# Three fp32r products for the unshifted channels, and a denominator shared out over ScalarE and GpSimd, in a recurrent layer with a selected transformer block

## The chip, the cores and the metric

The kernel runs on one core of a Trainium2 chip. The metric is the device time of one execution in microseconds; a kernel is run several times and the median is taken. The engines are TensorE (PE, with its weight loads shown apart as PEld), VectorE (DVE), ScalarE (ACT), GpSimd (POOL) and SyncE (SP), which issues most of the transfers. Each executes its own instructions in the order in which they are written, and they wait for each other through semaphores.

## The reference, cut to what matters

The input is x of 32 sequences, 512 tokens and 256 channels. The first layer mixes each channel with a neighbour in time, but only for the lower half of the channels: `xx` equals `x` in channels 128 to 255, so that there `xk`, `xv` and `xr` are all plain `x`.

```
xx = concat([x shifted forward [:64], x shifted back [64:128], x[128:]])
xk = x * mix_k + xx * (1 - mix_k)          # xv, xr likewise
k, v, r = xk @ Wk.T, xv @ Wv.T, xr @ Wr.T
for t:                                     # w = spatial_decay / T, u = spatial_first / T
    out_t = (a + exp(u + k_t) * v_t) / (b + exp(u + k_t))
    a, b = a * exp(w) + exp(k_t) * v_t, b * exp(w) + exp(k_t)
x = layernorm(x + (sigmoid(r) * out) @ Wo.T)
```

Behind it stands a second block: a router weighs each token, the 63 heaviest tokens of each sequence go through RMS norm, attention with rotary positions and an MLP (GELU, 1024 wide), and the result is put back and normed.

## The kernel before

Channels lie on the 128 partitions in CC = 2 halves (c = 0: the shifted ones, c = 1: the unshifted ones), and the T = 512 tokens of a sequence lie along the free dimension. The kernel has three parts: a loop over the 32 sequences (to about 500 us), 16 pairs of sequences in attention (to about 728 us), and an MLP over 8 groups of tokens.

The loop is software-pipelined. Each engine has its own `period(at)`, which lists by hand what it does in the period of sequence n, for sequences n+1 down to n−3. In the words below, K, V and R are the three projections of a sequence, each in two PSUM banks.

- TensorE: `projections(n)` waits for `mixed(n)` and does K, V and R (L766): for each, two output halves by two channel halves, 12 fp32 products of 512 columns, each recorded as two instructions. Then `outputs(n-1)` waits for the gate `g_ready(n-1)`, and adds x (transposes, L779) and the output projection (L781). In some periods from n = 19 on, `selection(n)` adds small products (`weights_turn`, `slots_turn`, and `picks`, L822 and L826, in n = 28 and 29).
- ScalarE: `exp_k_of(n)`, two exponentials of K, one to SBUF (L1111), one in place in PSUM (L1113); `reciprocal_of(n-1)` (L1132) waits for `sum_done(n-1)`; `differences_scaled(n+1)` (L1140) writes three scaled copies into `xm` and signals `scaled`; `variances_of(n-2)` (L1153 to L1155); `exp_r_of(n)` (L1117); `ln_den_of(n)` (L1123); `ln_gate_of(n)` (L1127); `evacuation_of(n-1)` (L1148); `rows_of(n-3)` (L1160), which writes the normed rows.
- GpSimd: `differences_of(n+1)` (L548); `gate_of(n-1)` (L570) waits for `num_done` and `rec_done` of n−1; `mixes_of(n+1)` (L554), three additions behind `scaled(n+1)`, signals `mixed(n+1)`; `scale_of(n-2)` raises the variance to the power −1/2 (L577) and computes the offsets of the norm (L579, L580); `log_sum_of(n)` (L561).
- VectorE: `den_scan_of(n)` (L1431), two scans that give b, with the decay read from the tile `ewb`, in which exp(w) stands 512 times per channel; `den_of(n)` (L1445), two sums exp(u) · exp(k) + b; `products_of(n)` (L1438); `clamp_of(n)` (L1453); `num_of(n)` (L1458, L1463); then from n = 18 on the selection (top-k in rounds of eight, L1552 and L1554, one-hot matrices, L1590, scans with the column `ones` repeated, L1566 and L1571); then `statistics_of(n-1)` (L1472, L1483, L1487).

In attention, ScalarE and GpSimd still finish the norm of the last sequences between their other work. In the last loop period GpSimd also gathers a mask and norms the first tokens (`attention_begun`) ahead of the gate. The MLP already splits its operands into a rounded fp32r part and an fp32r rest, and does three fp32r products in place of one fp32 product (L1073, L1084).

Of the kernel before, what the change touches and what calls it, by code (L numbers as in the profile page):

```python
# [7 lines left out]
def rwkv_then_selected_block_kernel(nc, x_chan, w_attn, columns, mask_rows, positions,  # L8
# [20 lines left out]
    P = 128  # L29
# [30 lines left out]
    with ctx:  # L60
# [17 lines left out]
        ewb = sb("ewb", [P, CC, T])  # L78
# [84 lines left out]
        u_hi, u_lo = half_at(rest, FC, GP * P), half_at(rest + FC * GP * P, FC, GP * P)  # L163
        psK, psV, psR = ps[:, 0:2, :], ps[:, 2:4, :], ps[:, 4:6, :]
# [56 lines left out]
        sc = ewb.rearrange("p a (h k) -> p (a h) k", k=K)  # L221
# [38 lines left out]
        ewb_made = sem("ewb_made")  # L260
# [27 lines left out]
        t2_done = sem("t2_done")  # L288
        s2_done = sem("s2_done")
# [226 lines left out]
        def _(pool):  # L516
# [33 lines left out]
            def mixes_of(s):  # L550

                pool.wait_ge(scaled, s.n + 1)
                for m in range(3):
                    last = g.tensor_tensor(xm[s.par][:, m, :], xm[s.par][:, m, :], xs[s.k][:, :], ALU.add)  # L554
                last.then_inc(mixed, 1)

            def log_sum_of(s):
# [3 lines left out]
                g.tensor_tensor(ld[s.par][:, :, :], ld[s.par][:, :, :], er[s.par][:, :, :], ALU.add).then_inc(sum_done, 1)  # L561

# [85 lines left out]
            def period(at):  # L648
# [98 lines left out]
        def _(pe):  # L747
# [350 lines left out]
        def _(act):  # L1098
# [790 lines left out]
```

## Time and profile before

| What | Value |
|---|---|
| Median of 3 runs | 848.66 us (844.45 to 848.79) |
| The profiled execution | 843.93 us |
| Its span, first to last instruction | 841.9 us |
| Mean granted clock of TensorE | 0.963 |
| Busy: PE, DVE, ACT, POOL | 774.4, 677.3, 497.2, 508.8 us |

The busy times are unions over the whole span, so they average over the three parts of the kernel. The profiled execution is one run; the times of the rows come from it alone, and it is 4.7 us under the median of the others.

### The profile page before, as it was taken

What the parts mean: (1) busy time and instruction counts of PE and PEld (TensorE: products, weight loads), DVE (VectorE), ACT (ScalarE), POOL (GpSimd) and SP (SyncE); (2) the same over time, 40 slices, a digit from 0 to 9 for tenths busy, and PEclk for the clock granted to TensorE, in tenths of its full rate; (3) what the DMA queues carried; (4) which work ended last, traced back from release to release, by engine and by line L of the source; (5) the groups of instructions that cost most, each with busy time, mean ns of one, the idle gap of its engine ahead of it and who ended that gap; (6) DMA issues with size and microseconds to landing.
All of it is one profiled execution on the core that took longest, in us unless ns stands there. A gap on an engine that the chain in (4) does not pass through costs nothing.

```text
span 841.9 us, 12743 instructions
## 1 busy us (share of the span) xinstructions
PE 774.4 (92%) x4276; PEld 524.8 (62%) x4276; DVE 677.3 (80%) x1382; ACT 497.2 (59%) x908; POOL 508.8 (60%) x463
## 2 busy tenths in 40 slices
PE   6899999999999999999999986779998898899982
PEld 4455556565555556455456654567776777899982
DVE  5788988888888899999998996698698664258873
ACT  2557777868777786877765664555565666322210
POOL 1677878787887868788675894455464633102223
PEclk8999999999999999999999999899899997999996
DMA  8023242322223242232321111501010110000001
GB/s 218 1 62 114 63 126 62 111 76 95 92 69 119 62 122 67 87 102 63 110 78 63 44 57 54 160 27 45 26 36 22 39 52 2 1 1 14 26 26 37
DMA packets 37335, 55.37 MB, mean 66 GB/s; under 512 B 3360, under 2 KB 26528, under 8 KB 37280
## 3 DMA queue, kind: packets, MB, share of 16 engines
q1 hardware_dynamic: 34464, 46.28, 18.2%
q0 software_dynamic: 2816, 8.39, 3.3%
q8 instruction: 31, 0.51, 0.3%
q14 instruction: 24, 0.20, 0.1%
HBM read 35.78 MB, written 18.87 MB: 65 GB/s over the span
## 4 chain that ended last, share of the span: by engine, by line
PE 62%; DVE 21%; issue 7%; POOL 5%; ACT 3%; DMA 1%; SPq 0%; POOLq 0%; DVEq 0%; ACTq 0%
PE ps L766 26%; PE ps L781 9%; PE ps L1084 6%; PE ps L1073 6%; DVE arena L1431 3%; PE ps L961 2%; PE ps L779 2%; PE ps L894 2%; DVE arena L1483 2%; DVE arena L1463 2%; DVE arena L1458 2%; PE ps L969 2%; DVE arena L1453 2%; DVE arena L1472 2%; DVE ps L1438 1%
## 5 line engine op out<-in xcount | busy, mean ns | idle before, releaser
L766 PE MATMUL ps<-arena,wa 128*128 128x512 f32 x768 | 340.5, 599 | 9.9 <-DMA wa<-w_attn 5.1
L766 PEld LDWEIGHTS ps<-arena,wa 128*128 128x128 f32 x768 | 146.9, 192 | 184.4 <-issue 168.4
L781 PE MATMUL ps<-wa,arena 128*128 128x256 f32 x512 | 131.7, 380 | 0.0
L570 POOL TENSOR_TENSOR arena<-arena 128x1024 f32<-128x1024 f32 x32 | 75.8, 2367 | 87.2 <-issue 64.5
L554 POOL TENSOR_TENSOR arena<-arena 128x512 f32<-128x512 f32 x93 | 115.9, 1275 | 5.8 <-ACT arena L1140 5.8
L1431 DVE TENSOR_TENSOR_SCAN arena<-ewb,ps 128x511 f32<-128x511 f32 x64 | 74.5, 1205 | 24.5 <-ACT ps L1113 23.3
L781 PEld LDWEIGHTS ps<-wa,arena 128*128 128x128 f32 x512 | 87.3, 190 | 6.6
L561 POOL TENSOR_TENSOR arena<-arena 128x1024 f32<-128x1024 f32 x32 | 75.7, 2366 | 15.8 <-ACT arena L1127 15.8
L1458 DVE TENSOR_TENSOR_SCAN arena<-ewb,ps 128x511 f32<-128x511 f32 x64 | 74.1, 1199 | 0.0
L1160 ACT ACTIVATE arena<-arena 128x256 f32<-128x256 f32 x128 | 66.0, 589 | 0.0
L1117 ACT ACTIVATE ps<-ps 128x1024 f32<-128x1024 f32 x32 | 32.3, 1008 | 55.9 <-PE ps L766 55.9
L1140 ACT ACTIVATE arena<-arena,cols 128x512 f32<-128x512 f32 x93 | 60.0, 710 | 0.0
L577 POOL TENSOR_TENSOR arena<-arena,mhalf 128x8 f32<-128x8 f32 x32 | 53.2, 1661 | 7.5 <-ACT arena L1155 5.8
L627 POOL TENSOR_SCALAR arena<-arena,norm 128x256 f32<-128x256 f32 x16 | 15.3, 954 | 67.8 <-ACT norm L1255 67.7
L1453 DVE TENSOR_SCALAR arena<-ps 128x1024 f32<-128x1024 f32 x32 | 39.1, 1222 | 20.9 <-ACT ps L1117 20.9
L1339 ACT ACTIVATE arena<-ps 128x512 f32<-128x512 f32 x32 | 19.1, 598 | 61.1 <-PE ps L1073 61.1
L740 POOL TENSOR_TENSOR fst<-fst,mhalf 128x2 f32<-128x2 f32 x8 | 5.7, 716 | 81.7 <-DVE fst L1847 81.7
L779 PEld LDWEIGHTS ps<-ident,arena 128*128 128x128 f32 x256 | 35.9, 141 | 26.8 <-issue 15.8
L1084 PE MATMUL ps<-halves 128*128 128x256 f32 x384 | 49.0, 289 | 3.7 <-DVE halves L1818 3.7
L1111 ACT ACTIVATE arena<-ps 128x1024 f32<-128x1024 f32 x32 | 32.7, 1023 | 33.0 <-PE ps L766 33.0
L1084 PEld LDWEIGHTS ps<-halves 128*128 128x128 f32 x384 | 48.1, 198 | 3.9 <-DVE halves L1818 3.9
L779 PE MATMUL ps<-ident,arena 128*128 128x128 f32 x256 | 48.9, 273 | 0.5 <-POOL arena L570 0.5
(215 smaller groups left out, 1523.2 us busy)
## 6 DMA issues: line engine op xcount, KB each, us to landing
arena<-x_chan SPq DMA_DIRECT2D x32, 512.0 KB, 4.1
out<-arena SPq DMA_DIRECT2D x32, 512.0 KB, 3.3
arena<-x_chan SPq DMA_DIRECT2D x64, 127.8 KB, 3.3
wa<-w_attn SPq DMA_DIRECT2D x1, 1024.0 KB, 7.7
wa<-w_up SPq DMA_DIRECT2D x1, 1024.0 KB, 6.1
wa<-w_down SPq DMA_DIRECT2D x1, 1024.0 KB, 5.5
wqk<-w_qk SPq DMA_DIRECT2D x1, 512.0 KB, 4.8
wv<-w_v SPq DMA_DIRECT2D x1, 256.0 KB, 5.0
```

What stands on the lines that cost most here:

```text
L554: last = g.tensor_tensor(xm[s.par][:, m, :], xm[s.par][:, m, :], xs[s.k][:, :], ALU.add)
L561: g.tensor_tensor(ld[s.par][:, :, :], ld[s.par][:, :, :], er[s.par][:, :, :], ALU.add).then_inc(sum_done, 1)
L570: g.tensor_tensor(gg[s.par][:, :, :], num[s.par][:, :, :], ld[s.par][:, :, :], ALU.mult).then_inc(g_ready, 1)
L766: last = mm(bank[:, o, :], wa[:, m, c, o * P:(o + 1) * P], rhs, start=(c == 0), stop=(c == CC - 1))
L779: mm(psY[:, j, c * P:(c + 1) * P], xc[s.k][:, c, tokens], ident[:, :], is_transpose=True, start=(c == 0), stop=False)
L781: last = mm(psY[:, j, :], gg[s.par][:, c, tokens], wa[:, 3, c, :], start=False, stop=(c == CC - 1))
L1084: last = mm(ps[:, 4 + g.par, i * C:(i + 1) * C], x[:, f, i * P:(i + 1) * P], w[:, f, :], start=(f == 0 and t == 0), stop=(f == FC - 1 and ...
L1140: last = a.activation(xm[s.par][:, m, :], diff[:, :], ACT.Copy, scale=mix[:, m:m + 1])
L1160: last = a.activation(xt[s.k][:, j, :], xt[s.k][:, j, :], ACT.Identity, scale=stat[s.par][:, j, S2:S2 + 1], bias=nm[s.par][:, j:j + 1])
L1431: last = v.tensor_tensor_scan(bb[:, c, 1:T], ewb[:, c, 0:T - 1], psK[:, c, 0:T - 1], 0.0, ALU.mult, ALU.add)
L1453: v.tensor_scalar(er[s.par][:, :, :], psR[:, :, :], 2.0 ** 62, None, ALU.min).then_inc(clamp_done, 1)
L1458: v.tensor_tensor_scan(aa[:, c, 1:T], ewb[:, c, 0:T - 1], psV[:, c, 0:T - 1], 0.0, ALU.mult, ALU.add).then_inc(scan_a_done, 1)
```

## The change

It has five parts.

1. For the unshifted half (c = 1), which all three projections read as plain x, the weights and x are split into a part rounded to fp32r and the rest: `w1_hi` (ScalarE) and `w1_lo` (VectorE) once, `x1_hi` (ScalarE, in `differences_scaled`) and `x1_lo` (GpSimd, behind the three mixes, carrying the `mixed` signal now) for each sequence. One fp32 product becomes three fp32r products: hi·hi, hi·lo, lo·hi. Sequence 0 keeps the fp32 product. The half c = 0 stays fp32.
2. The power −1/2 of the norm is no longer GpSimd's `pow` but ScalarE's logarithm and exponential (`logs_of`, `roots_of`).
3. The second half of the denominator is taken from VectorE: ScalarE multiplies exp(k) by exp(u) (`den_part_of`, behind the reciprocal), and GpSimd adds b (`den_second_of`, between `gate_of` and `mixes_of`). `ln_den_of` waits for both halves. VectorE's next denominator scan waits for GpSimd's addition.
4. The scans read the decay as one column repeated (`euw[:, 1, c:c+1].to_broadcast`), and the tile `ewb` is gone; its place in SBUF (`late`) holds the product of part 3, and later the scores.
5. GpSimd does `scale_of` after `log_sum_of`, no longer before it.

```diff
 mixes_of (GpSimd)
                 for m in range(3):
-                    last = g.tensor_tensor(xm[s.par][:, m, :], xm[s.par][:, m, :], xs[s.k][:, :], ALU.add)
-                last.then_inc(mixed, 1)
+                    g.tensor_tensor(xm[s.par][:, m, :], xm[s.par][:, m, :], xs[s.k][:, :], ALU.add)
+                g.tensor_tensor(x1_lo[s.par], xc[s.k][:, 1, :], x1_hi[s.par].bitcast(fp32), ALU.subtract).then_inc(mixed, 1)
...
+            def den_second_of(s):
+                pool.wait_ge(eku_done, s.n + 1)
+                pool.wait_ge(scan_b_done, s.n + 1)
+                if s.had(2):
+                    pool.wait_ge(ld_done, s.n - 1)
+                g.tensor_tensor(den[s.par][:, 1, :], eku[:, :], bb[:, 1, :], ALU.add).then_inc(den1_done, 1)
...
 scale_of (GpSimd)
-                pool.wait_ge(t2_done, s.n + 1)
-                g.tensor_tensor(stat[s.par][:, :, S1:S2 + 1], stat[s.par][:, :, VE:VN + 1], mhalf[...], ALU.pow).then_inc(s2_done, 1)
...
 period (GpSimd)
                 if at.had(1) and at.back(1).exists():
                     gate_of(at.back(1))
+                if at.exists():
+                    den_second_of(at)
                 if nxt.exists():
                     mixes_of(nxt)
-                if at.had(2) and at.back(2).exists():
-                    scale_of(at.back(2))
                 if isinstance(at.n, int) and at.n == B - 1:
                     value_tiles_cleared()
                 if at.exists():
                     log_sum_of(at)
+                if at.had(2) and at.back(2).exists():
+                    scale_of(at.back(2))
...
 projections (TensorE)
                     for o in range(CC):
-                        for c in range(CC):
-                            rhs = xm[s.par][:, m, :] if c == 0 else xc[s.k][:, c, :]
-                            last = mm(bank[:, o, :], wa[:, m, c, o * P:(o + 1) * P], rhs, start=(c == 0), stop=(c == CC - 1))
+                        out_part = slice(o * P, (o + 1) * P)
+                        mm(bank[:, o, :], wa[:, m, 0, out_part], xm[s.par][:, m, :], start=True, stop=False)
+                        if isinstance(s.n, int) and s.n == 0:
+                            last = mm(bank[:, o, :], wa[:, m, 1, out_part], xc[s.k][:, 1, :], start=False, stop=True)
+                            continue
+                        for t, (w, x) in enumerate(((w1_hi, x1_hi), (w1_hi, x1_lo), (w1_lo, x1_hi))):
+                            last = mm(bank[:, o, :], w[:, m, out_part], x[s.par], start=False, stop=(t == 2))
...
+            def den_part_of(s):
+                act.wait_ge(ek_done, s.n + 1)
+                if s.had(1):
+                    act.wait_ge(den1_done, s.n)
+                a.activation(eku[:, :], ek[:, 1, :], ACT.Copy, scale=euw[:, 0, 1:2]).then_inc(eku_done, 1)
...
 ln_den_of (ScalarE)
                 act.wait_ge(den_done, s.n + 1)
+                act.wait_ge(den1_done, s.n + 1)
...
 differences_scaled (ScalarE)
                 for m in range(3):
-                    last = a.activation(xm[s.par][:, m, :], diff[:, :], ACT.Copy, scale=mix[:, m:m + 1])
-                last.then_inc(scaled, 1)
+                    a.activation(xm[s.par][:, m, :], diff[:, :], ACT.Copy, scale=mix[:, m:m + 1])
+                a.activation(x1_hi[s.par], xc[s.k][:, 1, :], ACT.Copy).then_inc(scaled, 1)
...
+            def logs_of(s):
+                act.wait_ge(t2_done, s.n + 1)
+                if s.had(2):
+                    act.wait_ge(rows_done, s.n - 1)
+                a.activation(stat[s.par][:, :, S1:S2 + 1], stat[s.par][:, :, VE:VN + 1], ACT.Ln).then_inc(logs_done, 1)
+            def roots_of(s):
+                act.wait_ge(logs_done, s.n + 1)
+                a.activation(stat[s.par][:, :, S1:S2 + 1], stat[s.par][:, :, S1:S2 + 1], ACT.Exp, scale=-0.5).then_inc(s2_done, 1)
...
 period (ScalarE)
                 if at.had(1) and at.back(1).exists():
                     reciprocal_of(at.back(1))
+                if at.exists():
+                    den_part_of(at)
                 if at.back(-1).exists():
                     differences_scaled(at.back(-1))
                 if at.had(2) and at.back(2).exists():
                     variances_of(at.back(2))
                 if at.exists():
                     exp_r_of(at)
+                if at.had(2) and at.back(2).exists():
+                    logs_of(at.back(2))
+                if at.exists():
                     ln_den_of(at)
+                if at.had(2) and at.back(2).exists():
+                    roots_of(at.back(2))
...
 attention (ScalarE, n == 1)
                     variances_of(At(0, B - 1))
                     rows_of(At(0, B - 3))
+                    logs_of(At(0, B - 1))
                     rows_of(At(0, B - 2))
+                    roots_of(At(0, B - 1))
...
 den_scan_of and den_of (VectorE)
+                if s.had(1):
+                    dve.wait_ge(den1_done, s.n)
...
-                    last = v.tensor_tensor_scan(bb[:, c, 1:T], ewb[:, c, 0:T - 1], psK[:, c, 0:T - 1], 0.0, ALU.mult, ALU.add)
+                    last = v.tensor_tensor_scan(bb[:, c, 1:T], euw[:, 1, c:c + 1].to_broadcast([P, T - 1]), psK[:, c, 0:T - 1], 0.0, ALU.mult, ALU.add)
...
-                for c in range(CC):
-                    last = v.scalar_tensor_tensor(den[s.par][:, c, :], psK[:, c, :], euw[:, 0, c:c + 1], bb[:, c, :], ALU.mult, ALU.add)
-                last.then_inc(den_done, 1)
+                v.scalar_tensor_tensor(den[s.par][:, 0, :], psK[:, 0, :], euw[:, 0, 0:1], bb[:, 0, :], ALU.mult, ALU.add).then_inc(den_done, 1)
```

## Rows read from the trace of the kernel before

**Rows 1.** The page's busy times (us, share of the span, instructions).

```profile
PE 774.4 (92%) x4276; PEld 524.8 (62%) x4276; DVE 677.3 (80%) x1382; ACT 497.2 (59%) x908; POOL 508.8 (60%) x463
```

**Rows 2.** Timeline of PE: start us, us, line, operation, count.

```profile
203.92 10.46 PE L766 MATMUL ps<-arena,wa 128*128 128x512 f32 x24
...
218.55 10.46 PE L766 MATMUL ps<-arena,wa 128*128 128x512 f32 x24
```

**Rows 3.** The chain that ended last, first and last of 17 equal blocks.

```profile
43.08 10.30 PE ps L766 x24
...
277.26 10.31 PE ps L766 x24
```

**Rows 4.** Busy time by stretch: PE, PEld, DVE, ACT, POOL, granted clock, DMA.

```profile
57.71:277.25 219.54, 219.54 (x722) 124.31 (x721) 188.95 (x391) 165.21 (x251) 173.61 (x136) 1.00 0.30 91
...
415.75:427.00 11.25, 11.25 (x40) 6.68 (x40) 10.97 (x24) 7.30 (x12) 9.50 (x8) 1.00 0.41 119
448.54:452.00 3.46, 3.46 (x6) 1.52 (x6) 3.30 (x14) 0.00 (x0) 0.47 (x1) 0.56 0.75 233
```

**Rows 5.** Timeline of ACT, DVE and POOL in the period of rows 2.

```profile
207.55 1.02 ACT L1111 ACTIVATE arena<-ps 128x1024 f32<-128x1024 f32 x1 [0.36 <-PE ps L766]
...
209.52 2.33 DVE L1431 TENSOR_TENSOR_SCAN arena<-ewb,ps 128x511 f32<-128x511 f32 x2 [0.97 <-ACT ps L1113]
...
210.45 1.94 ACT L1140 ACTIVATE arena<-arena,cols 128x512 f32<-128x512 f32 x3
210.76 2.36 POOL L570 TENSOR_TENSOR arena<-arena 128x1024 f32<-128x1024 f32 x1 [2.97 <-ACT arena L1132]
...
213.08 3.74 POOL L554 TENSOR_TENSOR arena<-arena 128x512 f32<-128x512 f32 x3
```

**Rows 6.** Timeline at the start of the loop.

```profile
22.82 3.72 POOL L554 TENSOR_TENSOR arena<-arena 128x512 f32<-128x512 f32 x3 [5.77 <-ACT arena L1140]
...
26.59 3.70 PE L766 MATMUL ps<-arena,wa 128*128 128x512 f32 x8 [0.88 <-POOL arena L554]
```

**Rows 7.** The chain that ended last, single steps of several lines.

```profile
400.76 1.21 DVE wseq L1566
...
445.74 0.44 PE ps L822 x4
...
460.72 0.87 PE ps L781 x4
...
752.06 5.76 PE ps L1084 x48
```

**Rows 8.** Groups by line: count, busy us, mean ns, idle before.

```profile
L554 POOL TENSOR_TENSOR arena<-arena 128x512 f32<-128x512 f32 x93 | 115.9, 1275 | 5.8 <-ACT arena L1140 5.8
...
L1445 DVE SCALAR_TENSOR_TENSOR arena<-ps,euw,arena 128x512 f32<-128x512 f32 x64 | 45.1, 746 | 3.2
```

**Rows 9.** Timeline of PE, the projections of sequences 28 and 31.

```profile
429.05 10.57 PE L766 MATMUL ps<-arena,wa 128*128 128x512 f32 x24
...
482.43 10.46 PE L766 MATMUL ps<-arena,wa 128*128 128x512 f32 x24
```

**Rows 10.** The chain that ended last, denominator scans, first and last of ten.

```profile
299.88 2.34 DVE arena L1431 x2
...
389.20 2.34 DVE arena L1431 x2
...
406.06 2.34 DVE arena L1431 x2
...
438.08 2.34 DVE arena L1431 x2
```

**Rows 11.** Timeline of DVE in the selection.

```profile
416.38 2.17 DVE L1571 TENSOR_TENSOR_SCAN wseq<-ones,wseq 16x512 f32<-16x512 f32 x1
```

**Rows 12.** Timeline of POOL in attention.

```profile
513.18 1.68 POOL L577 TENSOR_TENSOR arena<-arena,mhalf 128x8 f32<-128x8 f32 x1 [5.83 <-ACT arena L1155]
...
525.20 1.68 POOL L577 TENSOR_TENSOR arena<-arena,mhalf 128x8 f32<-128x8 f32 x1 [1.70 <-ACT arena L1160]
```

More of the change, by code:

```diff
@@ L77, in rwkv_then_selected_block_kernel @@
         euw = sb("euw", [P, 2, CC])
-        ewb = sb("ewb", [P, CC, T])
+        late = sb("late", [P, CC, T])
+        eku = late[:, 0, :]
         rwb = sb("rwb", [P, C])
@@ L163, in rwkv_then_selected_block_kernel @@
         u_hi, u_lo = half_at(rest, FC, GP * P), half_at(rest + FC * GP * P, FC, GP * P)
+        at_x = rest
+        x1_hi, x1_lo = ([halves[:, at_x + (2 * n + i) * T:at_x + (2 * n + i + 1) * T] for i in range(2)] for n in range(2))
+        w1_hi, w1_lo = (halves[:, at_x + 4 * T + n * 3 * C:at_x + 4 * T + (n + 1) * 3 * C].rearrange("p (m o) -> p m o", o=C) for n in range(2))
         psK, psV, psR = ps[:, 0:2, :], ps[:, 2:4, :], ps[:, 4:6, :]
@@ L220, in rwkv_then_selected_block_kernel @@
         kblk = [place(CC, 2 * P) for _ in range(2)]
-        sc = ewb.rearrange("p a (h k) -> p (a h) k", k=K)
+        sc = late.rearrange("p a (h k) -> p (a h) k", k=K)
         pT = both(H // 2, P)
@@ L288, in rwkv_then_selected_block_kernel @@
         t2_done = sem("t2_done")
+        logs_done = sem("logs_done")
+        den1_done = sem("den1_done")
+        eku_done = sem("eku_done")
+        w1_rounded = sem("w1_rounded")
+        w1_split = sem("w1_split")
         s2_done = sem("s2_done")
@@ L572, in scale_of @@
             def scale_of(s):
-                pool.wait_ge(t2_done, s.n + 1)
                 if s.had(2):
                     pool.wait_ge(rows_done, s.n - 1)
-                g.tensor_tensor(stat[s.par][:, :, S1:S2 + 1], stat[s.par][:, :, VE:VN + 1], mhalf[:, 0:2 * TJ].rearrange("p (j a) -> p j a", a=2), ALU.pow).then_inc(s2_done, 1)
                 pool.wait_ge(s2_done, s.n + 1)
@@ L756, in projections @@
                 pe.wait_ge(mixed, s.n + 1)
+                if isinstance(s.n, int) and s.n == 1:
+                    pe.wait_ge(w1_split, 1)
                 for m, bank, ready, used in ((0, psK, k_ready, den_done), (1, psV, v_ready, num_done), (2, psR, r_ready, clamp_done)):
@@ L1105, in _ @@
             act.wait_ge(consts_made, 4)
+            act.wait_ge(w_in, 16)
+            a.activation(w1_hi, wa[:, 0:3, 1, :], ACT.Copy).then_inc(w1_rounded, 1)
             def exp_k_of(s):
@@ L1110, in exp_k_of @@
                     act.wait_ge(ekv_done, s.n)
+                    act.wait_ge(eku_done, s.n)
                 a.activation(ek[:, :, :], psK[:, :, :], ACT.Exp).then_inc(ek_done, 1)
                 a.activation(psK[:, :, :], psK[:, :, :], ACT.Exp).then_inc(ekp_done, 1)
+            def den_part_of(s):
[3 more added lines that the diff above has]
+                a.activation(eku[:, :], ek[:, 1, :], ACT.Copy, scale=euw[:, 0, 1:2]).then_inc(eku_done, 1)
             def exp_r_of(s):
@@ L1326, in _ @@
             variances_of(At(0, B - 2))
+            logs_of(At(0, B - 2))
+            roots_of(At(0, B - 2))
             for n in range(1, NP + 4):
@@ L1419, in _ @@
             dve.wait_ge(rw_chain, 3)
-            dve.wait_ge(ewb_made, 1 + CC)
             dve.wait_ge(first_col, 2)
+            dve.wait_ge(w1_rounded, 1)
+            v.tensor_tensor(w1_lo, wa[:, 0:3, 1, :], w1_hi.bitcast(fp32), ALU.subtract).then_inc(w1_split, 1)
             def den_scan_of(s):
                 dve.wait_ge(ekp_done, s.n + 1)
+                if s.had(1):
+                    dve.wait_ge(den1_done, s.n)
                 if s.had(2):
@@ L1443, in den_of @@
                 dve.wait_ge(scan_b_done, s.n + 1)
-                for c in range(CC):
-                    last = v.scalar_tensor_tensor(den[s.par][:, c, :], psK[:, c, :], euw[:, 0, c:c + 1], bb[:, c, :], ALU.mult, ALU.add)
-                last.then_inc(den_done, 1)
+                v.scalar_tensor_tensor(den[s.par][:, 0, :], psK[:, 0, :], euw[:, 0, 0:1], bb[:, 0, :], ALU.mult, ALU.add).then_inc(den_done, 1)
             def clamp_of(s):
@@ L1457, in num_of @@
                 for c in range(CC):
-                    v.tensor_tensor_scan(aa[:, c, 1:T], ewb[:, c, 0:T - 1], psV[:, c, 0:T - 1], 0.0, ALU.mult, ALU.add).then_inc(scan_a_done, 1)
+                    v.tensor_tensor_scan(aa[:, c, 1:T], euw[:, 1, c:c + 1].to_broadcast([P, T - 1]), psV[:, c, 0:T - 1], 0.0, ALU.mult, ALU.add).then_inc(scan_a_done, 1)
                 if s.had(2):
```

4 lines of the change are left out of this document (removed).

## The prediction

> **What bounds the kernel now.** I read the page's totals first: TensorE (PE) is busy 92% of an 841.9 us span [rows 1]. That is an average over a recurrent loop (to about 500 us), attention (to 728) and the MLP, and the change touches almost only the loop, so I read one period of the loop. In the PE timeline the 24 projection matmuls of one sequence start at 203.92 and those of the next at 218.55 [rows 2], and the chain that ended last holds such blocks 14.64 us apart from 43 us on [rows 3]: (277.26 − 43.08)/16 = 14.636. The granted clock is 1.00 with PE busy all 219.54 us of that stretch [rows 4]. So the first half of the loop is pure PE time: 24 × 0.4287 = 10.29 (the block's 10.30) and 4.34 for the outputs. From n = 19 the selection's small VectorE (DVE) operations join in and the chain runs over DVE; K(28) starts at 429.05 [rows 9], 152.0 after K(18) at 277.06 (K(n) is the first projection matmul of sequence n).
>
> PE is not the only loop, though. mixed(n) starts K(n); K(n)'s bank lets ScalarE (ACT) do two exponentials and then `reciprocal_of(n-1)`; that lets GpSimd (POOL) do `gate_of(n-1)`, and behind it, in order, stand `mixes_of(n+1)`, which start K(n+1). In the same period: K at 203.92, ACT's first exponential at 207.55, the gate at 210.76, the mixes from 213.08 for 3.74, so to 216.82 [rows 2, 5]. That is 12.90, and PE takes up K(n+1) only at 218.55. The start of the loop shows this circle when PE does wait for it: mixes end at 22.82 + 3.72 = 26.54, K(1) starts at 26.59, 0.05 later [rows 6]. So the circle is 12.95 against PE's 14.64: 1.7 us in reserve, and it is what the change spends.
>
> **The change, part by part, for one period.**
>
> *Projections.* Half of the twelve fp32 products (12 of 24 instructions, 12 × 0.4287 = 5.14) become 18 fp32r products over 512 columns. No row shows one. In the MLP 48 fp32r products over 256 columns take 5.76 [rows 7], 0.120 each; a product over 512 columns is surely not shorter, so 0.120 is the floor and 0.240 (twice that) the ceiling. An fp32 instruction over 512 columns, which takes 0.4287, is a second neighbour: fp32 over 256 columns takes 0.87/4 = 0.217 [rows 7], 1.8 times the fp32r one, so 0.4287/1.8 = 0.238, or with exactly half 0.214. Small products of 16 columns pace at 0.44/4 = 0.11 [rows 7], so part of the 0.120 is weight loading, which 512 columns would hide. I take 0.220, near the half. PE's period: 14.64 − 5.14 + 18 × 0.220 = 13.46. K alone: 8 × 0.4287 = 3.43 becomes 4 × 0.4287 + 6 × 0.220 = 3.03, so 0.40 off the circle (0.27 to 0.43; 1.0 at the floor).
>
> The Trainium skill (TensorE: Matmul & The Clock Gate, section Back-to-back issue gap) gives 131 ns for a matmul of 512 columns in a sustained stream of weight load and matmul. The rows speak against it here: 256 columns alone take 0.120. By it K would take 2.50 and the circle below would be 0.53 shorter.
>
> *POOL.* Two operations are put on the circle. `den_second_of(n)` stands between gate and mixes: one 128x512 add, 1.24 (a mix takes 1275 ns, three of them 3.74, overlapping a little [rows 5, 8]). `x1_lo` stands behind the three mixes and carries `mixed` now: another 1.25. The `pow` of L577 (1.68) goes, but it stood behind the mixes, as log_sum does: that takes nothing off the circle.
> Neither wait of `den_second_of` ends late: scan_b ends some 2.4 after ACT's second exponential, the gate 3.6 after it.
>
> The Trainium skill (GPSIMD Engine Reference, section Engine selection) sends a two-input elementwise add to VectorE. The rows bear that out, 746 ns there against 1275 [rows 8]; by the rule the second half of the denominator would have stayed and the circle been 1.24 shorter.
>
> *ACT.* `den_part_of` and `x1_hi` are 0.65 each (three scalings take 1.94 [rows 5]), logs and roots about 0.1 to 0.2 each. Counted from the first exponential of K(n), L1140 begins at 2.90 and ends at 4.84; with both additions `scaled` comes at 6.14, and POOL reaches the mixes at 3.21 + 2.32 (the gate) + 1.24 = 6.77. They fit, with 0.6 us left. The whole engine: 165.21/15 = 11.0 busy per period before [rows 4], 12.6 after, under 15; POOL's 11.6 becomes 12.4. Ln, Exp and Copy alternate already in each period with no table load between, so I price none.
>
> *DVE.* One of two 746 ns sums goes: −0.70. The scan's repeated column replaces a tile: I price it at nothing; such a scan with `ones` took 1.21 us [rows 7], two of L1431 2.33 [rows 5]. DVE is busy 188.95 of 219.54 here [rows 4], idle 2.0 per period, 0.97 of it before the scan [rows 5], so the gain is hidden in the first half. Where DVE sets the pace, nine periods take 438.08 − 299.88 = 138.2 from scan to scan, 15.36 each, and the longest 16.86 (389.20 to 406.06) [rows 10].
>
> **The sum.** New circle: 12.95 − 0.40 (K) + 1.24 (den_second) + 1.25 (x1_lo) = 15.04, say 15.05. It exceeds PE's 13.46 and the old 14.64: the loop changes its bound from PE to POOL and each period grows by 0.41.
> Start: period 0 keeps fp32, ACT's exponentials end at 20.81, den_part takes 0.65, but POOL's den_second waits for the scan, which ended at 23.35, then 1.24 + 3.72 + 1.25: K(1) at 29.65 for 26.59. K(2) at 44.70 for 42.91: +1.8.
> To K(18): 16 × 0.41 = +6.6, so +8.4 in all.
> K(18) to K(28): 10 × 15.05 = 150.5. Without the 0.70 DVE's mean there is 14.66, under the circle, but the load is uneven (the longest still 16.16, 1.1 over), and what the long periods exceed is not given back by the short ones; between 0 and 4 us in all I take 2.5: 153.0 for 152.0, +1.0.
> K(28) to K(31) was 53.4 [rows 9], 17.8 a period, since `picks` lie on PE in two of them. There PE still binds and gains its 14.64 − 13.46 = 1.18; the third goes by the circle, as long as it was. The granted clock fell behind the picks (0.56 in 448.54 to 452 [rows 4]) and should again: −2.4.
> Tail: in period 31 POOL's mask gather and norms stand ahead of the gate and are pushed about 0.6 back by the later log_sum. In attention the two `pow` on the chain (513.18, 525.20 [rows 12]) go. The first saves 1.1 (1.68 for two short ACT operations). The second loses 0.8: the roots of sequence 31 now stand behind another `rows_of`, 2.0 of ACT. Net +0.3.
> 8.4 + 1.0 − 2.4 + 0.3 = +7.3: span 849.2. The profiled execution took 843.93, 2.0 over its span, so 851.2. The median of the runs is 848.66, 4.7 above that execution, for a cause no view shows; the lowest is 844.45. On the median the sum gives 856.0, and that is my time.
>
> **Rivals.**
> 1. *PE stays the bound* (faster). It decides if the circle is under 13.5, so 1.55 less than summed: as if den_second and one mix cost nothing. Then 13.46 for 14.64 over 26 periods, about −30 + a few for DVE's stage: 820 to 825. For it: PE's 92%. Against: the circle's 12.95 already stands before 2.49 of POOL is added. Chance 0.06.
> 2. *fp32r products of 512 columns near the floor* (no change or a little faster). At 0.120 K takes 2.43, the circle 14.45: −0.2 for +0.41 per period, 26 × 0.6 = 16 less: about 840. By the 131 ns that the Trainium skill's page (TensorE: Matmul & The Clock Gate, Back-to-back issue gap) states it would be 842. At least 10 us come off once a product takes under 0.155. Against: the 0.217 and 0.120 at 256 columns. Chance 0.06. That some other link of the circle is 0.3 shorter than summed (POOL's semaphore handling) gives 848: 0.08.
> 3. *Worse than the circle.* ACT's `scaled` misses its 0.6 us, POOL's adds meet two-input DVE work (once a scan with both inputs in SBUF took 2.17 for 1.21, beside a POOL add [rows 11]), or PE, idle for 1.6 us in each period, is granted the lower clock now and then: K at 1.2 GHz costs 3.0 more. A wait of PE of 1.7 just before 415.75 left the clock at 1.00 [rows 4], so few: 0.3 to 1 us per period, 863 to 880. Chance 0.12.
> 4. *The change does not do what it says*: if fp32r over 512 columns takes 0.4287 as fp32, PE's period is 17.2 and the time about 920. Chance 0.02.
>
> **How the numbers follow.** The likeliest, POOL's circle at 14.95 to 15.2 with 0 to 4 for DVE's stage and the runs' own spread of 4.5, holds 0.66 and reaches from 847 to 863. To leave out no more than 2 in 10 the range takes the near parts of rivals 2 and 3: 845 to 865. A measurement of this kernel can tell about 0.5%, 844.4 to 852.9. Slower: most of the likeliest, rivals 3 and 4, 0.65. Same: the low end of the likeliest and the 0.08 of rival 2, 0.24. Faster: rival 1 and the floor of rival 2 in most of its width, 0.11.
>
> **What the profile of the changed kernel would show.** Right: K blocks 15.05 apart up to n = 25, PE idle about 1.6 before each with POOL's last `mixes_of` line named as releaser, PE's busy share down to about 85%, POOL's operations from gate to x1_lo back to back (8.5 us), K's bank ready some 3.3 after its start. The fp32r products should pace at 0.214 to 0.24. Wrong: K blocks waiting for ACT or DVE, a gap between gate and den_second (a late scan), or between den_second and the mixes (a late `scaled`); PE without idle time at 13.5 would mean rival 1.

## The result, and the profile after

| | before | after |
|---|---|---|
| median of the runs compared (us) | 846.56 (844.05 to 848.79, 4 runs) | 864.55 (862.92 to 867.14, 4 runs) |
| profiled execution / its span (us) | 843.93 / 841.9 | 862.92 / 861.2 |
| K(n) to K(n+1), median of the periods from K(2) to K(18) (us) | 14.64 | 15.16 |

The ratio is 1.0216 [1.0167, 1.0265]: slower, by 1.7 to 2.7%. The forecast was 856.0, in 845 to 865.

As in the prediction, K(n) is the first projection matmul of sequence n, and period n runs from K(n) to K(n+1). DVE's stage is K(18) to K(28), in which VectorE also does the selection.

The page's busy times, after:

```profile
PE 754.7 (88%) x4462; PEld 560.8 (65%) x4462; DVE 665.7 (77%) x1348; ACT 538.9 (63%) x1036; POOL 536.9 (62%) x494
```

Against [rows 1] PE lost 19.7 us of work, POOL and ACT gained 28.1 and 41.7, and the span still grew by 19.3: the work taken off PE did not set the time. One period of the first half shows why. This is the timeline of all engines after, for the period that answers to [rows 2, 5] (lines left out lie on engines that end early):

```profile
194.28 1.12 PE L783 MATMUL ps<-arena,wa 128*128 128x512 f32 x2 [1.24 <-POOL halves L563]
...
199.55 1.14 ACT L1165 ACTIVATE arena<-arena,lnbias 128x1024 f32<-128x1024 f32 x1
...
200.91 2.37 POOL L586 TENSOR_TENSOR arena<-arena 128x1024 f32<-128x1024 f32 x1 [2.82 <-ACT arena L1165]
...
203.04 0.62 ACT L1174 ACTIVATE halves<-arena 128x512 fp32r<-128x512 f32 x1
203.25 1.27 POOL L577 TENSOR_TENSOR arena<-late,arena 128x512 f32<-128x512 f32 x1
...
204.48 3.75 POOL L562 TENSOR_TENSOR arena<-arena 128x512 f32<-128x512 f32 x3
...
208.18 1.27 POOL L563 TENSOR_TENSOR halves<-arena,halves 128x512 fp32r<-128x512 f32 x1
...
209.51 1.12 PE L783 MATMUL ps<-arena,wa 128*128 128x512 f32 x2 [1.30 <-POOL halves L563]
```

Read it as a circle: K starts at 194.28; ACT's reciprocal (L1165) starts 5.27 later; the gate (L586), `den_second` (L577), the mixes (L562) and `x1_lo` (L563) stand one behind the other on POOL from 200.91 to 209.45 without a gap; K(n+1) starts 0.06 behind them. Before each K, PE idles 1.2 to 1.3, and L563 is named as its releaser. `x1_hi` (L1174), with which ACT signals `scaled`, ends at 203.66, before the mixes begin.

In the second half the same circle breaks now and then. PE's timeline after, at K(19) and at the three K that come late:

```profile
300.43 1.12 PE L783 MATMUL ps<-arena,wa 128*128 128x512 f32 x2 [1.23 <-POOL halves L563]
...
316.92 2.07 PE L783 MATMUL ps<-arena,wa 128*128 128x512 f32 x2 [2.12 <-POOL halves L563]
...
351.17 2.07 PE L783 MATMUL ps<-arena,wa 128*128 128x512 f32 x2 [3.57 <-POOL halves L563]
...
431.26 2.08 PE L783 MATMUL ps<-arena,wa 128*128 128x512 f32 x2 [3.99 <-POOL halves L563]
```

POOL's timeline after, ahead of the first late K, and one line of a later place (L569 log_sum, L556 differences, L586 gate, L577 `den_second`):

```profile
300.32 2.37 POOL L569 TENSOR_TENSOR arena<-arena 128x1024 f32<-128x1024 f32 x1
...
303.06 1.32 POOL L556 TENSOR_TENSOR arena<-arena 128x512 f32<-128x512 f32 x1
306.97 2.39 POOL L586 TENSOR_TENSOR arena<-arena 128x1024 f32<-128x1024 f32 x1 [2.59 <-issue]
310.65 1.27 POOL L577 TENSOR_TENSOR arena<-late,arena 128x512 f32<-128x512 f32 x1 [1.29 <-issue]
...
431.18 2.34 POOL L569 TENSOR_TENSOR arena<-arena 128x1024 f32<-128x1024 f32 x1
```

DVE's timeline after, in the same two places (L1560 and L1563 weigh the tokens, L1621 chooses the slots, L1523 is statistics, L1484 the scan of the denominator):

```profile
300.61 2.22 DVE L1560 TENSOR_TENSOR weights<-stats_all 128x64 f32<-128x64 f32 x1
...
303.27 1.20 DVE L1563 TENSOR_SCALAR weights<-weights,rbb 128x64 f32<-128x64 f32 x1
...
305.00 1.40 DVE L1523 BATCH_NORM_STATS2 arena<-arena 128x6 f32<-128x256 f32 x4
...
308.19 2.33 DVE L1484 TENSOR_TENSOR_SCAN arena<-euw,ps 128x511 f32<-128x511 f32 x2
...
431.46 2.60 DVE L1621 SCALAR_TENSOR_TENSOR wseq<-wsrc,topv,wseq 16x512 f32<-16x512 f32 x1
```

The gate ends at 309.36, but `den_second` starts at 310.65: it waits for the scan, which ends at 310.52. The scan is late because DVE's selection operations and statistics stand ahead of it, and two of the former were long: L1560 took 2.22 and L1563 1.20, while the next operation of L1560's shape, L1561, took 0.28, and L1563's counterpart before 0.28. Both end about 0.1 after the POOL operation beside them: 302.83 against 302.69, 304.47 against 304.38. L1621 too took 2.60, beside L569 and the small operation behind it; 0.73 before.

Such meetings are not new. The kernel before, at K(19) (PE, then DVE, then POOL's gate):

```profile
291.74 10.46 PE L766 MATMUL ps<-arena,wa 128*128 128x512 f32 x24
...
293.32 1.10 DVE L1509 TENSOR_TENSOR weights<-stats_all 128x64 f32<-128x64 f32 x1
...
299.88 2.33 DVE L1431 TENSOR_TENSOR_SCAN arena<-ewb,ps 128x511 f32<-128x511 f32 x2
...
298.50 2.37 POOL L570 TENSOR_TENSOR arena<-arena 128x1024 f32<-128x1024 f32 x1 [2.94 <-issue]
```

The same add took 1.10 and ended 0.14 after POOL's log_sum, which ended at 294.28. The scan began 8.14 after K(19) and ended at 302.21, 1.34 after the gate (300.87). In after it begins 7.76 behind K(19). So the scan is no later against its K than it was; what is new is that POOL, and with it K(n+1), waits for it. The other two late places are alike: the scans of 21 and 26 begin 8.8 and 9.2 behind their K in after, 9.5 and 10.3 before.

The Trainium skill (SBUF — State Buffer, section SBUF: two separate sides) says that a DVE operation with two SBUF inputs and a GpSimd operation that reads SBUF exclude each other for the whole instruction, and that one in a 2-port perf mode is shut out in the same way. The trace agrees for two inputs, 2.22 for 0.28 beside POOL's 2.37. L1563 has one tensor and a column as inputs and was held as well; in which mode it ran, no view shows.

The windows behind each late K (us, busy of PE, PEld, DVE, ACT, POOL, then the granted clock, DMA share, GB/s), and the first half of the loop:

```profile
316.92:320.30 3.38, 3.38 (x6) 2.06 (x7) 3.28 (x9) 1.18 (x4) 3.38 (x4) 0.51 0.51 155
320.30:324.00 3.70, 3.70 (x13) 2.17 (x12) 2.10 (x15) 2.03 (x3) 0.40 (x1) 0.99 0.73 212
351.17:354.30 3.13, 3.13 (x5) 1.83 (x6) 3.06 (x9) 0.69 (x2) 3.13 (x4) 0.50 0.48 150
...
431.26:434.40 3.14, 3.14 (x5) 1.83 (x6) 3.10 (x3) 0.71 (x2) 3.14 (x4) 0.50 0.47 148
...
57.69:280.00 222.31, 204.75 (x790) 136.44 (x791) 174.63 (x371) 180.36 (x306) 181.21 (x146) 1.00 0.30 90
```

PE idle for 1.2 to 1.3 in every period keeps 2.4 GHz over the whole first half; behind idle times of 2.12, 3.57 and 3.99 it works at 1.2 GHz (0.51, 0.50, 0.50) for over 3 us.

**Where the 19.3 us are.** K(18) starts at 285.28, 8.2 later than before (277.10). K(18) to K(28): 285.28 to 448.91 = 163.6, 11.7 more (before: 277.10 to 429.05 = 151.95). K(28) to K(31): 50.8, 2.6 less. K(31) to the end: 861.2 − 499.73 = 361.5, 2.0 more. That is 19.3. Each of these figures comes from one execution.

### The profile page after: what moved, and what is told of

Its sections match the earlier page's. It is cut to its first block and busy times, and to the rows that moved or that the text cites. A ratio compares the mean times of both kernels' runs of the same rounds, so it can differ in the third digit from the quotient of the medians.

```text
span 861.2 us, 13340 instructions
## 1 busy us (share of the span) xinstructions
PE 754.7 (88%) x4462; PEld 560.8 (65%) x4462; DVE 665.7 (77%) x1348; ACT 538.9 (63%) x1036; POOL 536.9 (62%) x494
## 5 line engine op out<-in xcount | busy, mean ns | idle before, releaser
L783 PE MATMUL ps<-arena,wa 128*128 128x512 f32 x384 | 205.3, 617 | 46.9 <-POOL halves L563 43.7
L788 PE MATMUL ps<-halves 128*128 128x512 f32 x558 | 240.0, 539 | 0.0
L788 PEld LDWEIGHTS ps<-halves 128*128 128x128 f32 x558 | 108.2, 194 | 101.1 <-issue 92.5
L586 POOL TENSOR_TENSOR arena<-arena 128x1024 f32<-128x1024 f32 x32 | 76.3, 2383 | 87.7 <-issue 71.5
L783 PEld LDWEIGHTS ps<-arena,wa 128*128 128x128 f32 x384 | 71.7, 194 | 74.9 <-POOL halves L563 55.2
L562 POOL TENSOR_TENSOR arena<-arena 128x512 f32<-128x512 f32 x93 | 116.1, 1281 | 0.0
L1484 DVE TENSOR_TENSOR_SCAN arena<-euw,ps 128x511 f32<-128x511 f32 x64 | 74.5, 1206 | 50.4 <-ACT ps L1138 49.2
L1136 ACT ACTIVATE arena<-ps 128x1024 f32<-128x1024 f32 x32 | 32.8, 1024 | 74.1 <-PE ps L788 71.3
L569 POOL TENSOR_TENSOR arena<-arena 128x1024 f32<-128x1024 f32 x32 | 76.2, 2381 | 0.0
L1509 DVE TENSOR_TENSOR_SCAN arena<-euw,ps 128x511 f32<-128x511 f32 x64 | 74.1, 1200 | 0.0
L1181 ACT ACTIVATE arena<-ps 128x1024 f32<-128x1024 f32 x32 | 32.7, 1022 | 29.1 <-PE ps L803 29.1
L1106 PEld LDWEIGHTS ps<-halves 128*128 128x128 f32 x384 | 48.1, 198 | 3.9 <-DVE halves L1869 3.9
```

Source lines behind the costliest of these rows:

```text
L586: g.tensor_tensor(gg[s.par][:, :, :], num[s.par][:, :, :], ld[s.par][:, :, :], ALU.mult).then_inc(g_ready, 1)
L783: mm(bank[:, o, :], wa[:, m, 0, out_part], xm[s.par][:, m, :], start=True, stop=False)
L788: last = mm(bank[:, o, :], w[:, m, out_part], x[s.par], start=False, stop=(t == 2))
L1106: last = mm(ps[:, 4 + g.par, i * C:(i + 1) * C], x[:, f, i * P:(i + 1) * P], w[:, f, :], start=(f == 0 and t == 0), stop=(f == FC - 1 and ...
L1484: last = v.tensor_tensor_scan(bb[:, c, 1:T], euw[:, 1, c:c + 1].to_broadcast([P, T - 1]), psK[:, c, 0:T - 1], 0.0, ALU.mult, ALU.add)
L1509: v.tensor_tensor_scan(aa[:, c, 1:T], euw[:, 1, c:c + 1].to_broadcast([P, T - 1]), psV[:, c, 0:T - 1], 0.0, ALU.mult, ALU.add).then_inc(sc ...
```

## The experiments

The kernel called "before" ran beside each, and each ratio is to it. The periods are medians of the first half of the loop, from the profiled executions.

**1. a_den_back: both halves of the denominator on VectorE again.**

```diff
-                if at.exists():
-                    den_part_of(at)        # ACT
-                if at.exists():
-                    den_second_of(at)      # POOL
-                v.scalar_tensor_tensor(den[s.par][:, 0, :], ...)
+                for c in range(CC):
+                    last = v.scalar_tensor_tensor(den[s.par][:, c, :], ...)
```

The waits for the two go with them, also the one of VectorE's next scan.

> The changed kernel with both halves of the denominator on VectorE again (the sums by ScalarE and GpSimd taken out, the rest of the change kept). If the circle through GpSimd sets the period of 15.16 us, it loses 1.24 us and K blocks of the first half stand 13.9 us apart; VectorE gets its 0.70 back and sets the pace from n = 19 on, so about 825 to 832 us in all. If the loop is slow for another reason (fp32r products, ScalarE's added work), the period stays within 0.3 of 15.16 and the time above 855.

Measured: 837.87, ratio 0.9897 [0.9866, 0.9929], period 13.93, so 1.23 less than 15.16. One POOL add is one add of period. The time is a miss, 6 above the range expected: the stage from K(18) to K(28) took 153.6, far from ten circles (139).

**2. b_rest_early: the two halves of x1 off the circle.** `x1_hi` is made at the end of ACT's period before, `x1_lo` ahead of the gate, while POOL waits anyway. `mixed` comes with the third mix again, and TensorE waits for `x1_lo` by a semaphore of its own. Nothing is left out.

```diff
-                a.activation(x1_hi[s.par], xc[s.k][:, 1, :], ACT.Copy).then_inc(scaled, 1)
-                g.tensor_tensor(x1_lo[s.par], ..., ALU.subtract).then_inc(mixed, 1)
...
                 if nxt.exists():
                     differences_of(nxt)
+                    rests_of(nxt)          # x1_lo, ahead of gate_of
...
+                if at.back(-2).exists():
+                    rounded_of(at.back(-2))   # x1_hi, end of ACT's period
```

> The changed kernel with x1_hi rounded at the end of ScalarE's period before and x1_lo taken by GpSimd ahead of the gate, where it was idle; no work is removed. Circle theory: x1_lo leaves the circle, period 15.16 - 1.25 = 13.9 in the first half, 826 to 836 us in all. If it is GpSimd's or ScalarE's load that counts and not the order, the time stays at 863.

Measured: 831.02, ratio 0.9792 [0.9759, 0.9826], period 13.93. POOL's timeline in it (L592 gate, L583 den_second, L564 mixes, L569 x1_lo):

```profile
201.90 2.39 POOL L592 TENSOR_TENSOR arena<-arena 128x1024 f32<-128x1024 f32 x1 [1.46 <-issue]
204.24 1.28 POOL L583 TENSOR_TENSOR arena<-late,arena 128x512 f32<-128x512 f32 x1
205.47 3.74 POOL L564 TENSOR_TENSOR arena<-arena 128x512 f32<-128x512 f32 x3
...
213.05 1.29 POOL L569 TENSOR_TENSOR halves<-arena,halves 128x512 fp32r<-128x512 f32 x1
```

POOL does as much as in after; only the add's place changed, from behind the mixes into POOL's idle time ahead of the gate (2.82 there became 1.46), and 1.23 of each period went. This kernel beats both the changed one and the one before.

**3. c_both: 1 and 2 together.**

> Both edits together. Circle theory: the circle falls to about 12.7 us, under TensorE's own 13.63 (6 x 1.549 for the projections and 4.34 for the outputs), so TensorE is the bound again with no idle time: period 13.6 to 13.7 in the first half, 818 to 828 us in all. Rival (some other link takes over at once, ScalarE's 12.6 us of work or VectorE): 13.9 or more, as in the single edits.

Measured: 834.18, ratio 0.9860 [0.9826, 0.9895], period 13.66 with PE never idle: PE's own period, 14.64 − 5.14 + 18 × 0.231 = 13.66. The time is a miss, 6 above the range expected: K(18) comes at 259.64, K(28) at 414.29, 154.7 later and more than before's 152.0. In DVE's stage the shorter circle brought nothing; that it is DVE's load is argued, not shown.

**4. d_stats_first: VectorE's statistics ahead of its selection work.** The order of the two in a period, nothing else.

```diff
-                if isinstance(at.n, int):
-                    selection(at.n)
                 if at.had(1) and at.back(1).exists():
                     statistics_of(at.back(1))
+                if isinstance(at.n, int):
+                    selection(at.n)
```

> The changed kernel with VectorE's statistics ahead of its selection work in each period. In the changed kernel the selection's operations with two SBUF inputs start with GpSimd's log_sum and take up to 2.6 us for 0.7. If that meeting is what makes the scans late from n = 19 to 27 (12 us over 15.16 per period, half of it the lower granted clock behind the longer waits), K(18) to K(28) shrinks from 163.6 to 152 to 158 us and the time is 852 to 858 us; the first half stays at 15.16. If it is only the amount of selection work, no change: 863 us, within 2.

Measured: 857.77, ratio 1.0141 [1.0094, 1.0187]; the interval overlaps that of the changed kernel (1.0167 to 1.0265). The period is 15.15 up to K(26) and K(18) to K(28) takes 151.8, 11.9 less than in after: the late scans are gone, and the low clock with them, and POOL's `den_second` follows the gate at once:

```profile
300.25 2.37 POOL L569 TENSOR_TENSOR arena<-arena 128x1024 f32<-128x1024 f32 x1
...
306.89 2.39 POOL L586 TENSOR_TENSOR arena<-arena 128x1024 f32<-128x1024 f32 x1 [2.72 <-issue]
309.24 1.28 POOL L577 TENSOR_TENSOR arena<-late,arena 128x512 f32<-128x512 f32 x1
```

1.6 come back at K(30) to K(31) (16.77 for 15.14), and K(31) to the end is 366.6 for 361.5. The order is changed in period 31 too, where the last rounds of the top-k (L1603, L1605) now stand behind the statistics; whether that costs the 5.1 was not tried.

**5. e_warm: matmuls without use in PE's three long waits.** 9, 15 and 17 small products ahead of the projections of 20, 22 and 27; they change no result.

```diff
+                    if at.n in (19, 21, 26):
+                        pe.wait_ge(den_done, at.n + 1)
+                        keep_warm(0, {19: 9, 21: 15, 26: 17}[at.n])
```

> The changed kernel with 9, 15 and 17 small products of no use (128x128, into the K bank once it has been read) on TensorE in the three long waits before K(20), K(22) and K(27), whose first products the changed kernel did at a granted clock of 0.50. The late scans stay as they are. If the lower clock is what makes K(20), K(22) and K(27) slow and with them the periods 20, 22 and 27 (16.77, 16.74 and 17.65 for 15.16), these fall to 15.2 to 15.4 and 4 to 5.5 us are gone: 857 to 860 us. If those periods are long because of VectorE alone, no change: 863, within 2.

Measured: 864.30, ratio 1.0233 [1.0164, 1.0303]. The four times are 858.5, 858.9, 869.7 and 870.4: two lie in the range expected, two 10 above it, and the trace is of the slowest. Periods 20 and 22, 16.77 and 16.74 in after, are 15.16 and 15.15; the periods ahead of them, with the late scan, stay at 16.50 and 17.49. PE's timeline there:

```profile
321.47 1.13 PE L783 MATMUL ps<-arena,wa 128*128 128x512 f32 x2
...
336.63 1.13 PE L783 MATMUL ps<-arena,wa 128*128 128x512 f32 x2 [1.24 <-POOL halves L563]
```

K(20) starts with a product time of 1.13, for 2.07 in after. So the late scans of 19 and 21 cost twice: their own delay, and then 1.6 for a K at 1.2 GHz. Period 27 stayed long (17.52) though the clock behind K(27) was 1.00: there the scan, 8.83 behind K(27), is late enough by itself. The profiled execution shows no gain. In it K(0) to K(2) took 34.44 (31.20 in after), with a clock of 0.50 from the start of K(0) (1.00 in after) and again behind K(1) (0.66), which the edit does not touch. Period 28 took 20.61 (17.70), and this does hang on the edit: with K(27) at full speed PE waited 2.56 ahead of K(28), for 0.68 in after, and the clock behind K(28) was 0.62, for 1.00.

**6. f_twice: `den_second` done twice.** One more 128x512 add of POOL on the circle; the second result is the one used.

```diff
+                g.tensor_tensor(spare[:, :], eku[:, :], bb[:, 1, :], ALU.add)
                 g.tensor_tensor(den[s.par][:, 1, :], eku[:, :], bb[:, 1, :], ALU.add)
```

> The changed kernel with GpSimd's den_second done twice (the first time to a tile that nobody reads): 1.24 us more of the same kind on the circle. Circle theory: each period that the circle sets grows by 1.24 to 16.40; TensorE's periods 28 and 29 take it up in part, about 27 x 1.24: 892 to 898 us. If only part of GpSimd's time is on the path, less than 0.6 per period: under 880.

Measured: 911.15, ratio 1.0841 [1.0785, 1.0897]. Periods of 16.39 (15.16 + 1.23, as expected) stand beside periods of 17.7 to 18.1. PE's timeline shows how they differ, by the first product's time:

```profile
200.60 1.13 PE L785 MATMUL ps<-arena,wa 128*128 128x512 f32 x2 [2.47 <-POOL halves L564]
...
216.99 2.08 PE L785 MATMUL ps<-arena,wa 128*128 128x512 f32 x2 [2.47 <-POOL halves L564]
...
234.87 1.12 PE L785 MATMUL ps<-arena,wa 128*128 128x512 f32 x2 [2.51 <-POOL halves L564]
```

With 2.5 idle in each period the clock falls in 6 of the 15 from K(2) to K(16): the first product takes 1.95 to 2.08 for 1.13, and the period is 1.3 to 1.7 longer. Six such periods are about 9 of the 13 by which the time lies above the range expected. After's 1.25 of idle time in each period was never followed by a lower clock from K(2) to K(18).

**7. i_early_stats: 2 and 4 together.**

> x1_lo ahead of the gate (as in b_rest_early) and VectorE's statistics ahead of its selection work (as in d_stats_first). If the two causes add, the period is 13.92 in the first half and stays there to K(27), since VectorE's own work is about 12.05 plus 1.5 to 4.1 and no longer meets log_sum: K(18) to K(28) from 155.1 to 140 to 145 us; with the end of the loop and attention as in b_rest_early, 818 to 826 us. If the order of VectorE pays only by giving back waits that the slower loop had, 829 to 833.

Measured: 827.89, ratio 0.9831 [0.9805, 0.9858], between the two ranges expected. The period is 13.93 and K(18) to K(28) 148.3, the shortest of all, but not ten periods of 13.93 (139), while 4 held its own 15.15 through the stage. Some of the held operations only moved ahead of the scan, to where POOL's gate runs (L592; L1637 is a DVE operation that takes 0.74 alone). The timeline of DVE, then POOL:

```profile
385.27 2.58 DVE L1637 SCALAR_TENSOR_TENSOR wseq<-wseq,need 16x512 f32<-16x512 f32 x1
387.88 2.33 DVE L1502 TENSOR_TENSOR_SCAN arena<-euw,ps 128x511 f32<-128x511 f32 x2
```

```profile
384.63 2.68 POOL L592 TENSOR_TENSOR arena<-arena 128x1024 f32<-128x1024 f32 x1 [1.48 <-issue]
390.34 1.27 POOL L583 TENSOR_TENSOR arena<-late,arena 128x512 f32<-128x512 f32 x1 [3.04 <-issue]
```

**8. j_all_order: 7, and `den_second` behind the mixes.**

```diff
-                if at.exists():
-                    den_second_of(at)
                 if nxt.exists():
                     mixes_of(nxt)
+                if at.exists():
+                    den_second_of(at)
```

> As i_early_stats, and GpSimd's den_second behind the mixes, which takes it off the circle through the gate: that circle falls to about 12.7. But ln_den then waits for an addition that ends 13.9 after K, log_sum and the reciprocal of the next period behind it. If TensorE's 13.63 is the next bound, 812 to 820; if the new circle (gate, mixes, den_second, ln_den, ln_gate, log_sum, reciprocal: about 14.4) binds, the period is 14.2 to 14.5 and the time 5 to 12 over i_early_stats.

Measured: 879.88, ratio 1.0435 [1.0414, 1.0455], the worst order but for the doubled add. Off the one circle the add lengthens another: den_second, ln_den, ln_gate, log_sum, the reciprocal, the gate, the outputs. Periods near 14.3, 15.9 and 17.6 come mostly in turn. PE no longer waits ahead of K but ahead of the outputs, with the gate (L592) as releaser, and behind some of these waits the clock falls, here at 242.18. PE's timeline in two periods (four output products of L812 take 1.03, or 1.56 and 1.91):

```profile
226.23 0.44 PE L810 MATMUL ps<-ident,arena 128*128 128x128 f32 x2 [1.93 <-POOL arena L592]
226.51 1.03 PE L812 MATMUL ps<-wa,arena 128*128 128x256 f32 x4
...
242.18 0.44 PE L810 MATMUL ps<-ident,arena 128*128 128x128 f32 x2 [2.08 <-POOL arena L592]
242.46 1.56 PE L812 MATMUL ps<-wa,arena 128*128 128x256 f32 x4
...
244.24 1.91 PE L812 MATMUL ps<-wa,arena 128*128 128x256 f32 x4
```

A circle of 14.3 was worked out beforehand, and that is the shortest period; that the others are longer shows that a second circle through the gate is not the whole account, and it stays open why three kinds take turns.

**9. k_back_stats: 3 and 4 together.**

> Both sums of the denominator on VectorE, x1_lo ahead of the gate (as in c_both), and statistics ahead of the selection work. The circle is 12.7 and TensorE's 13.65 binds the first half. From n = 19 a late scan no longer holds GpSimd's den_second, mixes and K, so no wait of TensorE behind it; VectorE's own 12.75 plus the selection sets the pace. If meetings with GpSimd were what c_both lost from n = 25 on (20.75 and 23.71 for two periods), 3 to 8 us less than c_both: ratio to the kernel before about 0.977 to 0.982. If VectorE's load alone sets this stage, as c_both: 0.986.

Measured: 832.36, ratio 0.9881 [0.9845, 0.9917]: a miss. Period 13.66 as in 3, K(18) to K(28) 151.3 instead of 154.7. That is 3.3 gained in this stage, and none of it in the ratio, which is that of VectorE's load alone (0.986 expected). The times spread in two pairs, 829.0 twice, 835.7 and 836.3, and the trace is of a fast one. DVE's stage still has long operations beside POOL. DVE's timeline, then POOL's (L592 gate, L564 mixes):

```profile
379.36 2.37 DVE L1628 TENSOR_SCALAR ties<-topv 16x63 f32<-16x63 f32 x1
381.76 2.22 DVE L1629 TENSOR_TENSOR_SCAN wseq<-ones,wseq 16x512 f32<-16x512 f32 x1
```

```profile
379.27 2.42 POOL L592 TENSOR_TENSOR arena<-arena 128x1024 f32<-128x1024 f32 x1 [1.14 <-issue]
381.65 5.09 POOL L564 TENSOR_TENSOR arena<-arena 128x512 f32<-128x512 f32 x3
```

L1628 takes 0.24 elsewhere and three mixes 3.75. How much of the 151.3 is such meetings and how much DVE's plain load this run does not part.

**10. n_pow_back: `pow` on GpSimd again**, behind log_sum, instead of ACT's logs and roots.

> The changed kernel with the power of the norm on GpSimd again, behind log_sum, and ScalarE's logarithms and roots out. GpSimd's 1.66 us lie in the 2.7 us in which it waits for the reciprocal, off the circle: the first half stays at 15.16. In attention the two steps of the last sequences change by 1 us or so. Theory: as the changed kernel within 3 us (ratio 1.018 to 1.026). If GpSimd's whole load counted, +1.6 per period: 905.

Measured: 864.98, ratio 1.0257 [1.0236, 1.0278] for after's 1.0216 [1.0167, 1.0265], period 15.15: no difference that these intervals show. POOL's 1.68 stands off the circle, behind the mixes before and behind log_sum here. K(18) to K(28) took 160.1 in this trace, with DVE's order as in after (163.6).

**11. g_column: the kernel before with the repeated column alone.**

```diff
-  v.tensor_tensor_scan(bb[:, c, 1:T], ewb[:, c, 0:T - 1], psK[:, c, 0:T - 1], ...)
+  v.tensor_tensor_scan(bb[:, c, 1:T], euw[:, 1, c:c + 1].to_broadcast([P, T - 1]), psK[:, c, 0:T - 1], ...)
```

> The kernel before with the scans reading the decay as one repeated column, nothing else changed (the tile is still made). Theory: the scan runs at the same 1.205 us and the time stays within 0.5% of before. If a repeated column were slower or faster to read, the scans in the trace differ from 1.2 us and the stage from n = 19 on, which VectorE paces, moves by four scans times ten periods times the difference.

Measured: 843.92, ratio 1.0003 [0.9993, 1.0014]. Nothing, as priced; a scan takes 1.20 with a column and with a tile.

## Why the prediction was right, and where its sizes were off

**The bound moved from PE to POOL's circle: right, shown.** Forecast 15.05 per period, measured 15.16. Experiments 1, 2 and 6 take one POOL add off the circle or put one on, by 1.23 each per period; in 2 and 6 the other work is the same, in 1 the sum goes back to VectorE. Rival 1 (PE stays the bound) would need a period of 13.66, which only appears once both adds are gone (3).

**The start: mis-sized, and hidden by luck.** K(18) was to come 8.4 later and came 8.2 later, but by two misses that cancel. K(2) was to come 1.8 later and came 0.4 earlier, at 42.52 for 42.91. The 16 periods behind it, forecast at 0.41 more each and +6.6, gave 8.6: they take 15.17 in the mean, since some are 15.23 to 15.26. The start differs for a reason that the sum left out: in before PE worked K(0), from 12.29 to 16.00, at a clock of 0.50, and ACT's first exponential came at 18.95; in after K(0) began at 11.32, its clock was 1.00, and the exponential came at 15.06. The clock at this place is not the change's doing: in the trace of 5, with the same code there, K(0) began at 0.50 too and K(0) to K(2) took 34.44 for 31.20. Why it differs stays open.

**fp32r over 512 columns: right in kind.** Three such products and two fp32 instructions repeat every 1.55 to 1.56. PE's timeline after:

```profile
302.54 1.26 PE L788 MATMUL ps<-halves 128*128 128x512 f32 x3
...
304.10 1.26 PE L788 MATMUL ps<-halves 128*128 128x512 f32 x3
```

So it is (1.55 − 0.857)/3 = 0.231 each, for 0.220 assumed. That puts K at 1.71 + 1.39 = 3.10, 0.07 more than summed, and is most of the 0.11 between 15.05 and 15.16. The 131 ns of the Trainium skill (TensorE: Matmul & The Clock Gate, Back-to-back issue gap) does not hold for fp32r at this size here; rival 2 is out.

**POOL's place for x1_lo, the pow, the column: right.** 1.25 to 1.27 for the first, nothing for the others (10, 11).

**DVE's stage: the term that was mis-sized most.** "between 0 and 4 us in all I take 2.5: 153.0 for 152.0". Measured 163.6. Ten measured periods are 151.6, so the stage's own excess was 12.0, not 2.5 nor within 4; in the trace of 10, with the same order on DVE, it was 8.5. It has two parts, by the periods: those with a late scan (19, 21, 26: 16.49, 17.48, 17.91) hold 1.33 + 2.32 + 2.75 = 6.4; those behind them (20, 22, 27: 16.77, 16.74, 17.65) hold 1.61 + 1.58 + 2.49 = 5.7. The step that failed: "Neither wait of `den_second_of` ends late" was read from the first half and used for the whole loop. In DVE's stage the scan stands behind the selection and ended 1.2, 2.2 and 2.6 after the gate in the three late periods. The trace before showed it already: there the scans of 19, 21 and 26 ended 1.3, 2.7 and 3.3 after the gate, and nothing on POOL waited for them. The prediction counted DVE's load per period against the circle, and not this new link between the two. Rival 3 named the meeting of POOL's adds with DVE and the low clock; it was given 0.12, and its 863 to 880 holds the 864.55, though by a few dear periods, not by "0.3 to 1 us per period". Its "K at 1.2 GHz costs 3.0 more" was too much: behind K(20) and K(22) the lower clock cost 1.6 (experiment 5).
That the order on DVE lets it happen is shown: 4 changes it alone and 11.9 of the 12.0 go. That the lower clock is a part of its own is shown for periods 20 and 22 by 5; for period 27 it is not.
That the long DVE operations come from POOL's log_sum beside them rests on their ends, 0.1 apart, in the traces. It was not tried with log_sum elsewhere and all else kept, and since the kernel before has such meetings too, how much of the 6.4 they make is open.

**K(28) to K(31)**: 50.8 for 51.0 forecast. **The tail**: +2.0 for +0.3. K(31) to the end was 361.5 in after, 364.4 in 5 and 355.1 in 6, whose code there is after's but for the doubled add; the 1.7 are within that spread, and the cause stays open.

**The sum**: 8.2 + 11.7 − 2.6 + 2.0 = 19.3, against +7.3 forecast; 10.7 of the 12.0 missing are DVE's stage. The time came out only 8.5 over the forecast because most of the 4.7 added for the median's distance from the profiled execution was not there: after's median is 1.6 above its own (864.55 − 862.92). That the 864.55 lies inside 845 to 865 is luck: with the 4.7 it would have been 867.6.

**Which version to keep.** With the fp32r split, 2 (0.9792 [0.9759, 0.9826]) and 7 (0.9831 [0.9805, 0.9858]) are both faster than before, by 1.8 to 2.4% and by 1.4 to 2.0%; their intervals overlap, so they are not told apart.

## What to carry to other kernels

An engine that is busy 92% may have a second circle right behind it: add up one turn, from K to K, over all engines in their order, before taking work off the busy one and giving it to a link of that turn. A helper step that depends on no fresh data belongs into the idle time of its engine, ahead of what it waits for, not behind the last link: with the same 1.25 us add behind the last link each period was 15.16, and ahead of the gate 13.93, for 14.64 before. A new wait ties two engines together: look in the old trace at when its two ends fall, in every stage. A wait read as harmless in one stage has to be read again in each stage whose engine is loaded differently.

## What the runs showed of the hardware

- PE's granted clock stayed at 1.00 with 1.2 to 1.3 us of waiting in each period; behind waits of 2.12, 3.57 and 3.99 it was 0.50 to 0.51. With 2.5 in every period it fell in 6 of 15.
- An fp32r product over 512 columns paces at 0.231 us, over 256 at 0.120 [rows 7], an fp32 instruction over 512 at 0.4287.
- Small DVE operations beside a POOL add of 128x1024 took 2.2 to 2.6 instead of 0.24 to 0.74, and once POOL's three adds 5.09 instead of 3.75: by the traces either side can be the one that waits.
